# k and v of a convolutional attention block computed by minimal filtering F(2,3) along the image rows

## The reference, cut to what matters

```python
inp = x + 2.0 * sinu                  # x already normalised over the channels
q = conv2d(inp, wq)                   # 1x1, 128 -> 256
k = conv2d(inp, wk, 1, 1)             # 3x3, padded by 1
v = conv2d(inp, wv, 1, 1)             # 3x3, padded by 1
q, k, v = (split_heads(q), split_heads(k), split_heads(v))   # 8 heads of 32
q = q * cos + rotate_every_two(q) * sin
k = k * cos + rotate_every_two(k) * sin
attn = jax.nn.softmax(jnp.einsum('bhid,bhjd->bhij', q, k) * SCALE, axis=-1)
attn = jnp.einsum('bhij,hg->bgij', attn, mix)
out = jnp.einsum('bhij,bhjd->bhid', attn, v)
```

## Time and profile before

| | |
|---|---|
| median of three runs | 3073.14 us |
| the profiled execution | 3079.39 us, span 3077.7 us |
| PE busy | 2957.6 us, 96% of the span |
| DVE busy | 2147.5 us, 70% |
| ACT busy | 1448.3 us, 47% |
| POOL busy | 1331.9 us, 43% |
| mean granted TensorE clock | 0.985 of full |

### The profile page before, as it was taken

How to read it: one execution, slowest core, us unless ns; L and a number is a source line. 1 busy time by engine, 2 the same in 40 slices (tenths; PEclk the granted TensorE clock), 3 DMA queues, 4 the chain that set the end, 5 groups by cost and what they waited for, 6 DMA issues and landing times.

```text
span 3077.7 us, 54491 instructions
## 1 busy us (share of the span) xinstructions
PE 2957.6 (96%) x20354; PEld 2723.8 (89%) x20354; DVE 2147.5 (70%) x3316; ACT 1448.3 (47%) x1862; POOL 1331.9 (43%) x996
## 2 busy tenths in 40 slices
PE   8999999999999999999999999999999999958996
PEld 6999889998999899988999899979998899946776
DVE  4677668775877487766877587748776687655663
ACT  2455335542555255534554355525553455435671
POOL 3244414542454334542464245433454246236783
PEclk9999999999999999999999999999999999969998
DMA  3364010101110101101010111010110111137665
GB/s 113 134 228 157 9 37 22 44 11 35 28 33 25 36 22 23 40 19 28 22 45 10 35 32 29 24 36 22 24 40 19 28 29 44 61 111 253 225 222 206
DMA packets 71429, 196.94 MB, mean 64 GB/s; under 512 B 16136, under 2 KB 16722, under 8 KB 71158
## 3 DMA queue, kind: packets, MB, share of 16 engines
q1 hardware_dynamic: 62070, 176.40, 18.7%
q0 software_dynamic: 9088, 16.94, 1.7%
HBM read 40.43 MB, written 63.34 MB: 34 GB/s over the span
## 4 chain that ended last, share of the span: by engine, by line
PE 88%; ACT 3%; issue 3%; DMA 2%; DVE 2%; SPq 1%; POOL 1%; POOLq 0%; ACTq 0%; DVEq 0%
PE PV L641 48%; PE ST L641 25%; PE MX L641 13%; DMA wt<-wall 2%; ACT h L1016 1%; ACT xr L1016 1%; PE PV L729 0%; DMA wall<-yrows 0%; ACT E L1016 0%; PE PV L772 0%; POOL yrows L609 0%; SPq L441 0%; DVE El L1318 0%; DVE mcol L1313 0%; PE MX L749 0%
## 5 line engine op out<-in xcount | busy, mean ns | idle before, releaser
L527 POOL TENSOR_TENSOR acc<-acc,tmp 128x256 f32<-128x256 f32 x512 | 802.8, 1568 | 1380.8 <-DVE tmp L1328 1380.8
L641 PE MATMUL PV<-vh,El 128*128 128x258 f32 x4096 | 1185.2, 289 | 11.8 <-DVE vl L1308 7.7
L641 PE MATMUL PV<-vh,Eh 128*128 128x258 f32 x4096 | 1154.5, 282 | 0.0
L641 PE MATMUL PV<-vl,Eh 128*128 128x256 f32 x4096 | 1149.6, 281 | 0.0
L1016 ACT ACTIVATE Eh<-ST 128x1024 fp32r<-128x1024 f32 x512 | 525.2, 1026 | 765.1 <-PE ST L641 765.1
L1313 DVE TENSOR_REDUCE mcol<-MX 128x1 fp32r<-128x1024 f32 x512 | 626.0, 1223 | 349.9 <-PE MX L641 347.1
L641 PEld LDWEIGHTS PV<-vh,El 128*128 128x128 f32 x4096 | 772.4, 189 | 43.2 <-DVE El L1318 8.8
L641 PEld LDWEIGHTS PV<-vl,Eh 128*128 128x128 f32 x4096 | 778.0, 190 | 24.5 <-issue 3.8
L641 PEld LDWEIGHTS PV<-vh,Eh 128*128 128x128 f32 x4096 | 772.6, 189 | 0.0
L1318 DVE TENSOR_TENSOR El<-E,Eh 128x1024 fp32r<-128x1024 f32 x512 | 632.2, 1235 | 9.9 <-ACT E L1016 9.8
L1016 ACT ACTIVATE E<-ST 128x1024 f32<-128x1024 f32 x512 | 522.3, 1020 | 0.0
(11 more groups left out here) (226 smaller groups left out, 3064.0 us busy)
## 6 DMA issues: line engine op xcount, KB each, us to landing
rows<-xr SPq DMA_DIRECT2D x68, 520.0 KB, 5.6
kst<-src SPq DMA_DIRECT2D x192, 128.0 KB
qst<-src SPq DMA_DIRECT2D x192, 128.0 KB
wt<-wall SPq DMA_DIRECT2D x39, 514.0 KB
wt<-wall SPq DMA_DIRECT2D x39, 512.5 KB
xrow<-rows SPq DMA_DIRECT2D x39, 260.0 KB
wall<-yrows SPq DMA_DIRECT2D x32, 256.0 KB, 4.8
xr<-in_x_dram SPq DMA_DIRECT2D x9, 512.0 KB, 3.5
```

What stands on the lines that cost most here:

```text
L527: nc.gpsimd.tensor_tensor(acc[:, ic, :], acc[:, ic, :], tmp[:, p, :], ALU.add).then_inc(s_acc, 1)
L641: return nc.tensor.matmul(o, w, m, start=start, stop=stop)
```

## The change

Along a row, two neighbouring outputs of a three-tap filter are computed from four products instead of six. Of the input row, even and odd pixels are combined into four components u0 to u3 of half the width (`mix_input`, on GpSimd, into `u32`, then split by `mixed_hi` and `mixed_lo` into `uh` and `ul`). Of each row of three taps, four mixed taps are made once in the setup (`outer_sums` on GpSimd, `middle_half` on ScalarE, `mix_weights` on VectorE). One component now needs three taps (the rows above, at and below), and four banks of products together give 512 even and 512 odd outputs: `middle_copy` on ScalarE and `middle_sums`, `even_odd` on VectorE combine them. `turn` is `even_odd` followed by the rotation.

```diff
+WINO = (1, 2, 0, 3)
...
+            def conv(b, cg, i):
+                comp, kind, cols = WINO[i], cg // 2, slice(cg % 2 * P, (cg % 2 + 1) * P)
+                if cg == 0:
+                    if i == 0:
+                        pe.wait_ge(s_uin, 2 * b + 2)
+                    pe.wait_ge(s_rf, b * 8 + i + 1)
+                elif i == 0:
+                    pe.wait_ge(s_mc, b * 4 + cg)
+                elif i == 1:
+                    pe.wait_ge(s_ms, b * 4 + cg)
+                else:
+                    pe.wait_ge(s_eo, b * 8 + 2 * cg + i - 3)
+                o = conv_bank(i)
+                if kind == 0:
+                    inner, edge = slice(0, NB - HALFW), slice(HALFW, NB)
+                    wh, wl = (t[:, 0, :, comp, cols] for t in (wch, wcl))
+                    mh, ml = (t[:, comp, HALFW:HALFW + NB] for t in (uh, ul))
+                    mm(o, wh[:, 1, :], ml, True, False)
+                    mm(o, wl[:, 1, :], mh, False, False)
+                    split3(o[:, edge], wh[:, 0, :], wl[:, 0, :], mh[:, inner], ml[:, inner], False, False)
+                    split3(o[:, inner], wh[:, 2, :], wl[:, 2, :], mh[:, edge], ml[:, edge], False, False)
+                    mm(o, wh[:, 1, :], mh, False, True).then_inc(s_cv, 1)
+                else:
+                    for half in range(2):
+                        oh_ = o[:, half * INNER:(half + 1) * INNER]
+                        for dy in range(3):
+                            at = (2 * (cg - 2) + half) * P + dy * HALFW
+                            last = split3(oh_, uh[:, comp, at:at + P], ul[:, comp, at:at + P],
+                                          wch[:, 1, dy, comp, :], wcl[:, 1, dy, comp, :], dy == 0, dy == 2)
                     last.then_inc(s_cv, 1)
...
+            def mix_input(n):
+                even, odd = (ln_x.rearrange("p (y x two) -> p two y x", y=IMG, two=2)[:, i, :, :] for i in range(2))
...
+                nc.gpsimd.tensor_tensor(u[1], even, odd, ALU.add).then_inc(s_u, 1)
+                nc.gpsimd.tensor_tensor(u[2], odd, even, ALU.subtract)
...
+            def middle_copy(b, cg):
+                act.wait_ge(s_cv, b * 20 + 4 * cg + 5)
+                if cg in (1, 2):
+                    act.wait_ge(s_rf, b * 8 + 2 * cg + 4)
+                if cg == 3:
+                    act.wait_ge(s_vlo, b * 4 + 2)
+                copy(vt[1][:, :], conv_bank(0)).then_inc(s_mc, 1)
...
             def rot_hi(b, g):
-                kind, c, hf = g // 4, g % 4 // 2, g % 2
                 wait(act, s_rr, b * 8 + g + 1)
-                copy(src[:, 2 * kind, c, hf * NB:(hf + 1) * NB].bitcast(f32r), rot_a[g % 2]).then_inc(s_rhi, 1)
+                wait(act, s_sd[g % 2], b * 64 + 16 * (g // 2))
+                copy(rt[:, g % 2, 0, :].bitcast(f32r), rot_a[g % 2]).then_inc(s_rhi, 1)
...
+            def middle_sums(b, cg):
+                dve.wait_ge(s_cv, b * 20 + 4 * cg + 6)
+                dve.wait_ge(s_mc, b * 4 + cg + 1)
+                tt(vt[0][:, :], vt[1][:, :], conv_bank(1), ALU.add)
+                tt(vt[1][:, :], vt[1][:, :], conv_bank(1), ALU.subtract).then_inc(s_ms, 1)
...
+            def even_odd(b, cg, odd):
+                dve.wait_ge(s_cv, b * 20 + 4 * cg + 7 + odd)
+                dve.wait_ge(s_ms, b * 4 + cg + 1)
+                if odd == 0:
+                    tt(vt[0][:, :], conv_bank(2), vt[0][:, :], ALU.add).then_inc(s_eo, 1)
+                else:
+                    tt(vt[1][:, :], vt[1][:, :], conv_bank(3), ALU.subtract).then_inc(s_eo, 1)
...
+            def turn(b, g):
+                cg, odd = g // 2 - 2, g % 2
+                even_odd(b, cg, odd)
+                dve.wait_ge(s_rlo, b * 8 + g - 1)
+                dve.wait_ge(s_eo, b * 8 + 2 * cg + odd + 1)
+                tt(rot_a[odd], vt[odd][:, :], table(cos_sb, g), ALU.mult)
+                nc.vector.stream_shuffle(rot_s[odd], vt[odd][:, :], swap).then_inc(s_rf, 1)
...
             def input_lo(n):
                 wait(dve, s_xhi, n + 1)
...
+                dve.wait_ge(s_u, 2 * n + 2)
+                tt(xl[:, :], ln_x, f(xh[:, :]), ALU.subtract).then_inc(s_xin, 1)
...
+            def mixed_lo(n, h):
+                at = (slice(None), slice(2 * h, 2 * h + 2), slice(HALFW, HALFW + NB))
+                dve.wait_ge(s_uhi, 2 * n + h + 1)
+                tt(ul[at], u32[:, 2 * h:2 * h + 2, :], f(uh[at]),
+                   ALU.subtract).then_inc(s_uin, 1)
+
+            def mix_weights(i):
+                dve.wait_ge(s_wa, i + 1)
+                dve.wait_ge(s_wb, i + 1)
+                stt(mixed[i][:, 0, :, :], outer[i], 0.5, middle[i], ALU.mult, ALU.add)
+                stt(mixed[i][:, 1, :, :], outer[i], 0.5, middle[i], ALU.mult, ALU.subtract).then_inc(s_wtr, 1)
...
-                    sp.dma_start(f(kst[par][row * DH:(row + 1) * DH, :]), src[r:r + DH, part, c, :]).then_inc(s_stk[par], 16)
+                    sp.dma_start(f(kst[par][row * DH:(row + 1) * DH, :]), stk_d[part, c, r:r + DH, :]).then_inc(s_stk[par], 16)
...
+            def spill(b, g):
+                kind, c, hf = g // 4, g % 4 // 2, g % 2
+                wait(sp, s_rlo, b * 8 + g + 1)
+                sp.dma_start(stk_d[2 * kind:2 * kind + 2, c, :, hf * NB:(hf + 1) * NB].rearrange("a p t -> p a t"),
+                             rt[:, g % 2, :, :]).then_inc(s_sd[g % 2], 16)
```

More of the change, by code:

```diff
@@ L199, in build @@
         xrow = [keep(f"xrow{i}", [P, 4, ROW], f32) for i in range(XR)]
-        idx = [keep(f"idx{i}", [P, 4], u32) for i in range(XR)]
+        idx = [keep(f"idx{i}", [P, 4], ui32) for i in range(XR)]
         xnh = [keep(f"xnh{i}", [P, NB], f32r) for i in range(2)]
@@ L247, in build @@
         s_xin = sem("s_xin")
+        s_wa, s_wb, s_wtr = sem("s_wa"), sem("s_wb"), sem("s_wtr")
+        s_u = sem("s_u")
+        s_uhi = sem("s_uhi")
+        s_uin = sem("s_uin")
+        s_mc = sem("s_mc")
+        s_ms = sem("s_ms")
+        s_eo = sem("s_eo")
+        s_sd = [sem(f"s_sd{i}") for i in range(2)]
         s_cv = sem("s_cv")
@@ L403, in batch @@
                 x_next = x_d[nxt, :, :] if isinstance(b, int) else x_d[sp.snap(nxt), :, :]
+                for g in range(6):
+                    spill(b, g)
+                spilled(b, 3)
                 stacks(b, 0)
+                for g in range(6, 8):
+                    spill(b, g)
+                spilled(b, 4)
                 if not isinstance(b, int):
@@ L566, in pair @@
                         row_pair(prev)
+                    if b is not None and k == 5:
+                        mix_input(b + 1)
             def batch(b):
@@ L571, in batch @@
                 if isinstance(b, int):
-                    with pool.Fori(0, HEADS // 2) as hp:
+                    with pool.Fori(0, HEADS // 2 - 1) as hp:
                         pair(b * UNITS + hp * 8)
                 else:
-                    for hp in range(HEADS // 2):
+                    for hp in range(HEADS // 2 - 1):
                         pair(b * UNITS + hp * 8, b - 1, hp)
+                pair(b * UNITS + UNITS - 8, b=b)
+            outer_sums()
+            mix_input(0)
             batch(0)
@@ L801, in scores @@
                 wait(pe, s_ex, 2 * n + p - 1)
+                if first is not None and p == 0:
+                    pe.wait_ge(s_ms, first * 4 + 4)
+                if first is not None and p == 1:
+                    pe.wait_ge(s_eo, first * 8 + 8)
                 for j in range(4):
@@ L1115, in batch @@
                     out_hi(prev, 0)
-                for g in range(1, 4):
-                    rot_hi(b, g)
+                rot_hi(b, 1)
+                rot_hi(b, 2)
+                middle_copy(b, 0)
+                rot_hi(b, 3)
                 if prev is not None:
@@ L1456, in pair @@
                             take_max(n + 2, k + 2, p)
+                        if last and k == 6 and p == 0:
+                            prepare(b + 1, 7)
                         if last and k == 7:
                             if p == 0:
-                                prepare(b + 1, 7)
-                            else:
                                 input_lo(b + 1)
+                            mixed_lo(b + 1, p)
                         normalise(n, k, p, head)
@@ L1468, in pair @@
                             route(prev, slots + 4 * k + 2 * p + 1)
-                        if last and 2 <= k <= 6 and p == 0:
-                            prepare(b + 1, k)
+                        if last and 1 <= k <= 5 and p == 0:
+                            prepare(b + 1, k + 1)
             def batch(b):
@@ L1497, in batch @@
                 take_max(n, 0, 0)
-                v_lo(b, 0)
+                middle_sums(b, 2)
+                rot_lo(b, 7)
+                even_odd(b, 2, 0)
                 take_max(n, 0, 1)
-                v_lo(b, 1)
+                even_odd(b, 2, 1)
                 if prev is not None:
@@ L1503, in batch @@
                     nc.vector.memset(acc[:, :, :], 0.0)
+                v_lo(b, 0)
```

(6 more changed lines are left out.)

293 lines of the change are left out of this document (158 added, 135 removed).

## The result

| | before | changed |
|---|---|---|
| median of the runs, us | 3073.23 (3072.90 to 3080.31, 4 runs) | 3045.61 (3043.80 to 3047.46, 4 runs) |
| profiled execution / its span, us | 3079.39 / 3077.7 | 3044.30 / 3042.6 |
| first q matmul of batch 0 | 33.93 | 43.34 |
| stage of batch 0 | 62.80 | 57.70 |
| stage of batches 1 to 7, mean (least, most) | 71.48 (71.46, 71.50) | 63.57 (63.16, 64.58) |

The ratio is 0.9906 (95%: 0.989 to 0.992): faster by 29 us, 25 to 34, where I had said 49. The stage runs from the first q matmul to the first value matmul, "attention" from there to the next batch's first q matmul, and the period is the sum of both; I took them from the timeline of PE.

What follows compares the result with a forecast made beforehand. The stage was taken as TensorE-bound before, then bound by the in-order chain over VectorE, GpSimd, ScalarE and DRAM. 7 x (11.1 - 2.5 - 0.4) = 57 gained, 8.8 lost in batch 0: net 48.6, forecast 3024 us, range 2985 to 3055.

Steps and rivals of the forecast that it cites:

- TensorE's 21 us: Convolution stage: TensorE's stream falls by 10.3 (k) + 10.5 (v) + 0.2 (q) = 21 us per batch.
- the clock's 2.5 us: Half clock after TensorE's waits in the stage: 1.7 behind the stack wait, 0.8 behind the end gap, per batch.
- setup and batch 0: First q matmul 11 us later, batch 0's stage 2.6 us shorter; batch 0 is 8.8 us worse.
- last pair: Last two units of each batch, `prepare` one unit earlier: 0.4 us lost per batch, from 0 to 0.7.
- the chain up to `rot_lo(5)`: Batch 1's stage, VectorE, GpSimd and ScalarE in turn: q starts at 352.2, `rot_lo(5)` ends at 382.2.
- The way through DRAM: Stage, `rot_lo(5)` to stacked head 0: write to `stk` 4.0 us, issue 3.7, landing about 2.3; 10.1 in all.
- The clock behind the end gap: After the 3.1 us TensorE gap before the first value matmul: half clock perhaps costs 0.8 us per batch.
- The wait for the stack: Sign in batch 1's stage: TensorE waits 4 to 8 us before the first `max_scores`; 5.7 us written.
- All of TensorE's saving lands: Rival, all stages: 8 x 21 = 168 us less the setup's 11, 2916; chance 0.02, with milder form (2984) 0.09.
- The way through DRAM is the bound: Rival, stacks in all 8 batches: slower than before from 6.1 us extra; 10 us extra gives 3105; chance 0.08.
- Nothing to see: Rival, stage: the chain is 5 to 7 us longer than written, 3064 to 3082 us; chance 0.06.
- does not do what it says: Rival, convolution: 256-column matmuls with mixed weights are bound by weight loads; chance 0.01, inside the other rivals' chances.

Runs made afterwards that it cites:

- the run that filled the gap: Changed kernel with eleven unread products on TensorE in the gap ahead of each batch's first value product, from batch 1 on: ratio 0.9868.
- a direct stack: Changed kernel with head 0's stack written straight from rt on chip instead of through DRAM: ratio 0.9867.
- the direct stack and ScalarE's order: Changed kernel with head 0's stack straight from rt, and row_transposed ahead of middle_copy(2) and rot_hi(6) on ScalarE: ratio 0.9804.
- the joined kernel: Changed kernel with direct stack, ScalarE's order, first value products' end order and four smaller moves: median 2981.02 us, ratio 0.9705.

## Why the prediction was right in direction and range, and 20 us off in size

The time lies in the range, and the mechanism was the forecast one: of TensorE's 21 us the stage gave back 7.9, because the way over `rot_lo(5)`, DRAM and the stack comes last, with the wait for `row_transposed` close beside it. The sum was 48.6 us; the two profiled executions differ by 35.1. By its steps, with each part of the clock's 2.5 us at the place where it falls:

| step | forecast, us | measured, us |
|---|---|---|
| setup and batch 0 | +8.8 | +6.0 |
| stage, batches 1 to 7 (11.1 less 1.7 for the clock) | 7 x -9.4 | 7 x -7.9 |
| attention, batches 1 to 6 (last pair 0.4, clock 0.8) | 6 x +1.2 | 6 x +2.04 |
| batch 7's attention and the experts | +1.2 | +2.0 |

- **The step that failed is the chain up to `rot_lo(5)`**: 33.3 us after the first q matmul instead of 30.0. By `rot_lo(3)` it was 1.8 us late (18.1 instead of 16.3): the first rotation started 2.4 us after q, behind the second `mixed_lo` and the last normalisation, which I had costed at nothing as long as q itself could start. In batches 2 to 7 it started 3.2 to 3.5 us after q and `rot_lo(3)` was 2.7 to 2.9 late; the one batch that I wrote down was the earliest, as it had been in the kernel before (1.0 us after q, and 1.4 to 1.8 in batches 2 to 7). Another 1.4 came after it, where two VectorE steps took 1.27 and 1.82 us instead of 0.69, beside GpSimd. I had raised GpSimd's price for the contention, to 1.45 where its steps measured 1.34 and 1.49, and left VectorE's as it was. (That the 1.64 of the earlier trace rows, an add of 256 columns, served as a bound for steps of 512 was luck: their longest was 1.65.) The Trainium skill ("GPSIMD Engine Reference", 1. Specifications) says that the two share their memory interfaces, so it is no surprise on either side. How much VectorE pays, its rows had to show, and those of the kernel before did: in batch 1, whose first rotation is the first row here, `rot_lo(0)` took 1.10 us beside GpSimd, and `rot_lo(3)` 0.69 without.

```profile
353.25 0.69 DVE L1274 TENSOR_TENSOR E<-ST,cos_sb 128x512 f32<-128x512 f32 x1 [0.21 <-PE ST L641]
...
358.04 1.10 DVE L1281 TENSOR_TENSOR src<-E,src 128x512 fp32r<-128x512 f32 x1 [2.20 <-ACT src L1016]
...
368.33 0.69 DVE L1281 TENSOR_TENSOR src<-E,src 128x512 fp32r<-128x512 f32 x1 [1.85 <-ACT src L1016]
```

- **The way through DRAM was priced 2.3 us too high**: 7.8 us from the end of `rot_lo(5)` to the first `max_scores`, instead of 10.1. The write lands in 2.7 us where I took 4.0 from the earlier trace rows, and the transfers are issued 0.43 us apart instead of 0.60. By luck this hid a good part of the first error: the first `max_scores` was 1.0 us late in batch 1 and 1.95 on the mean of batches 1 to 7. Behind it nothing more was lost (21.5 us to the first value matmul, where I had 20.0 and 1.7 for the clock), and the old stage had been written 0.3 short. That leaves 1.5 per batch, and 7 x 1.5 is the largest miss of the sum, 10 us.
- **The clock behind the end gap was under-priced**: 0.8, "perhaps", where the run that filled the gap shows 1.86 on the mean of batches 1 to 6 (1.4 to 2.7). The row I leaned on the earlier trace rows was one restart of 3 us; in the changed kernel three of the eight batches show 0.50 over the whole 5 us behind the gap, and the others 0.66 to 0.68. The 1.7 behind the stack was right. The last pair takes 0.18 at most instead of 0.4. Together 0.84 per batch, 6 us. The Trainium skill ("TensorE: Matmul & The Clock Gate", HAM oscillation — how this bites in real kernels) describes a loop whose waits make TensorE restart throttled in each round; the traces agree, with a granted clock of 0.50 to 0.68 behind the end gap in each of the eight batches.
- **A wait was missing from the working**: that for `row_transposed`, which ended 1.1 to 1.3 us before the stack's. It cost the forecast nothing, but by my working a direct stack would have given back the whole stall; it gave 1.3 us.
- **Setup and batch 0** were 2.8 us better: q at 43.34 instead of 45.1, since `mix_input` ended sooner (33.5 instead of 35.8), and a stage of 57.70 instead of 59.4 with its part of the clock; against that, batch 0's attention grew by 1.7 instead of 1.2.

Of the signs that I had named, q at 42 to 48 and the spacing of 0.12 came. The wait for the stack did not reach 4 to 8 us: it was 3.37 in batch 1 and 3.1 on the mean of batches 1 to 7, where I had 5.7, since TensorE too came to it late (37.7 us after q instead of 34.4, in part behind the waits of 0.9 for VectorE). Batch 1's stage, 63.28, lies just above 61 to 63, and the half clock lasted at least 6.6 us there, not some three.

Between 35.1 and the medians' 27.6 lie 7.5 us that I do not explain by a step. The profiled execution of before lay at the upper end of its runs, and the experts' part scatters by 7 us; which transfer or wait there does so stays open.

**The rivals.** "All of TensorE's saving lands" is refuted, and more than refuted: k's matmuls could take 9 us less still at no gain. "The way through DRAM is the bound" was right in that each microsecond more there counts once per batch (3.0 for 3), and wrong in its price; its point of 6.1 us extra was not reached, and 3 us extra left 0.9987. "Nothing to see" and "does not do what it says" did not happen.

## What to carry to other kernels

When TensorE's work in a stage is cut, write down the chain over the other engines, and price a stall as its length plus the time at half clock behind it: 1.7 and 1.9 us here, per batch on the mean. Write down more than one batch, since the first of a loop may be the earliest. Before removing a wait, look for a second one beside it. A few unread matmuls in a gap tell what the clock alone costs, and a kernel with work left out tells which engine paces a stage; neither needs the final version.

## What the runs showed that I had not expected

- After a gap of 2.7 to 2.9 us on TensorE the granted clock of the changed kernel went to its lower level in all eight batches, and in three it stayed there for all of the next 5 us of dense matmuls. The length of the gap alone does not decide it: with the direct stack and ScalarE's order one batch of eight kept the full clock behind the same gap, and in the joined kernel two of eight fell behind a gap of 0.49. The first 5 us of attention in one such batch of each:

```profile
1060.42:1065.42 5.00, 5.00 (x39) 4.91 (x40) 2.90 (x5) 2.32 (x3) 0.00 (x0) 1.00 0.01 3
...
1044.13:1049.13 5.00, 4.75 (x22) 4.21 (x23) 3.32 (x4) 2.68 (x4) 0.00 (x0) 0.66 0.02 3
```

- VectorE's `rot_lo` and k's cosine product, of 512 columns and two inputs outside PSUM, took up to 1.82 us (1.03 on the median) where they overlap with a GpSimd operation, and 0.68 to 0.70 where they do not.
- 512 KB from on chip to DRAM (`stk`) landed in 2.7 us on the median, 512 KB the other way in 3.5 to 4.4 (`xr`, `xg`). They stand at different places, and no run compares them at the same one.
